# Eight of sixteen transposes moved from TensorE to 32x32 blocks on VectorE and a trip through DRAM

## The reference, cut to what matters

```python
x = x + 0.5 * ffn(layernorm(x))          # "first"
x = x + attention(layernorm(x))
x = x + 0.5 * ffn(layernorm(x))          # "second"

def ffn(x, W_fc, W_proj):
    h = square(relu(x @ W_fc.T))          # 128 -> 512
    y = h @ W_proj.T                      # 512 -> 128
    ...                                   # 5 spike steps on y, counted
    return count / 5

def attention(h, ...):                    # h has its own layer norm first
    keys, values = h @ Wk.T + bk, h @ Wv.T + bv
    w = exp((keys @ Wka.T + bka) / sqrt(128))
    w = w / cumsum(w, axis=1)
    return cumsum(w * keys, axis=1) * values
```

## Time and profile before

| what | value |
|---|---|
| median of 3 runs | 148.12 us (147.59 to 148.47) |
| the profiled execution | 147.76 us, span 146.0 us |
| TensorE | busy 140.3 us, 96% of the span |
| VectorE | busy 117.3 us, 80% |
| ScalarE | busy 113.8 us, 78% |
| GpSimd | busy 95.8 us, 66% |
| granted TensorE clock | 0.999 |

### The profile page before, as it was taken

One profiled execution on the slowest core, in us unless ns is written; L12 is line 12 of the kernel. 1 busy time (PEld: TensorE's weight loads), 2 busy tenths in 40 slices (PEclk: granted clock), 3 DMA queues, 4 the chain that ended last, 5 costly groups with the idle time before them and its releaser, 6 DMA issues.

```text
span 146.0 us, 2901 instructions
## 1 busy us (share of the span) xinstructions
PE 140.3 (96%) x945; PEld 126.1 (86%) x945; DVE 117.3 (80%) x403; ACT 113.8 (78%) x215; POOL 95.8 (66%) x141
## 2 busy tenths in 40 slices
PE   7899999999999999999999999999999999999990
PEld 7689898989989899998988989889789898979790
DVE  3894559388699989999779999999999978453674
ACT  3278877789896996959979697796796977977761
POOL 1439247929999929894998989989967952520300
PEclk9999999999999999999999999999999999999999
DMA  4975000000000000000000000020020102020222
GB/s 140 270 203 161 4 2 0 0 0 4 2 0 2 0 4 2 0 0 0 4 0 0 0 0 7 0 72 0 2 76 0 57 15 72 7 72 0 72 72 72
DMA packets 10510, 5.09 MB, mean 35 GB/s; under 512 B 1152, under 2 KB 10496, under 8 KB 10496
## 3 DMA queue, kind: packets, MB, share of 16 engines
q1 hardware_dynamic: 9808, 4.53, 10.7%
q10 hardware_dynamic: 688, 0.39, 0.9%
HBM read 2.82 MB, written 2.10 MB: 34 GB/s over the span
## 4 chain that ended last, share of the span: by engine, by line
PE 48%; DVE 25%; issue 14%; POOL 6%; DMA 3%; POOLq 1%; ACT 1%; ACTq 1%; DVEq 0%
PE work L932 19%; PE hidden L853 5%; PE hidden L857 5%; PE hidden L854 5%; POOL normed L386 4%; DMA proj_raw<-in_L_ffn_W_proj_dram 3%; DVE weight_sum L699 3%; PE work L866 2%; POOL rstd L380 2%; DVE stats L559 2%; DVE pooled L723 2%; DVE share_bank L713 2%; DVE weight_key L706 2%; DVE share_bank L718 2%; DVE stats_att L559 2%
## 5 line engine op out<-in xcount | busy, mean ns | idle before, releaser
L932 PE MATMUL work<-proj_t,square 128*128 128x128 f32 x480 | 61.2, 275 | 0.0
L932 PEld LDWEIGHTS work<-proj_t,square 128*128 128x128 f32 x480 | 58.8, 192 | 2.4 <-ACT square L460 0.4
L460 ACT ACTIVATE square<-relu 128x512 f32<-128x512 f32 x60 | 37.7, 641 | 0.7
L455 ACT ACTIVATE relu<-hidden 128x512 f32<-128x512 f32 x64 | 36.7, 606 | 0.1
L853 PE MATMUL hidden<-in_hi,fc_lo 128*128 128x512 f32 (+1 forms) x66 | 27.5, 417 | 0.1
L857 PE MATMUL hidden<-in_lo,fc_hi 128*128 128x512 f32 (+1 forms) x66 | 25.6, 387 | 0.0
L854 PE MATMUL hidden<-in_hi,fc_hi 128*128 128x512 f32 (+1 forms) x66 | 25.4, 385 | 0.0
L380 POOL TENSOR_TENSOR rstd<-var_eps,minus_half 128x4 f32<-128x4 f32 x15 | 15.2, 1012 | 14.7 <-DVE neg_mean L572 14.7
L632 DVE TENSOR_TENSOR in_lo<-work,in_hi 128x512 fp32r<-128x512 f32 x15 | 10.2, 680 | 12.3 <-ACT in_hi L451 12.3
L386 POOL TENSOR_SCALAR normed_att<-x_att,neg_mean_att,rstd_att 128x128 f32<-128x128 f32 x32 | 18.1, 578 | 0.8
L386 POOL TENSOR_SCALAR normed<-x_second,neg_mean,rstd 128x128 f32<-128x128 f32 x32 | 16.9, 540 | 0.8
(11 more groups left out here) (118 smaller groups left out, 245.8 us busy)
## 6 DMA issues: line engine op xcount, KB each, us to landing
x_first<-_attn_hidden_states_dram SPq DMA_DIRECT2D x7, 256.0 KB, 4.0
out_dram<-x_out SPq DMA_DIRECT2D x7, 256.0 KB, 2.2
out_dram<-x_out SPq DMA_DIRECT2D x4, 64.0 KB, 1.5
x_first<-_attn_hidden_states_dram ACTq DMA_DIRECT2D x1, 128.0 KB, 2.7
x_first<-_attn_hidden_states_dram SPq DMA_DIRECT2D x1, 128.0 KB, 2.4
fc_raw<-in_L_ffn_W_fc_dram SPq DMA_DIRECT2D x1, 128.0 KB, 2.8
fc_raw<-in_L_ffn_W_fc_dram ACTq DMA_DIRECT2D x1, 128.0 KB, 3.3
proj_raw<-in_L_ffn_W_proj_dram SPq DMA_DIRECT2D x1, 128.0 KB, 3.1
```

Source lines behind the costliest of these rows:

```text
L455: nc.scalar.activation(relu[j.lane][:, c, :], bank_of_hidden(j, c)[:], ACT.Relu).then_inc(relu_made[j.lane], 1)
L460: nc.scalar.activation(square[j.lane][:, c, :], relu[j.lane][:, c, :], ACT.Square).then_inc(squares_act[j.lane], 1)
L932: last = nc.tensor.matmul(work[j.lane][:, tokens], square[j.lane][:, c, tokens], proj_t[:, c, :], start=(c == 0 and t == 0), stop=(c == NC ...
```

## The change

Jobs of index 3 to 10 are no longer transposed by TensorE. When their `normed` is there, VectorE transposes its 32x32 blocks in one instruction (`ff_block_turn`) into `blocks`; SyncE stores the whole tile to DRAM (256 KB), waits until the store has landed, and issues four loads (one for each group of 32 partitions, 64 KB each, in runs of 512 bytes) which put the blocks in their places in `block_turned`. ScalarE's `in_hi` and VectorE's `in_lo` of these jobs read `block_turned` in SBUF, through a rearranged pattern, where they read `work` in PSUM. The step in which a job's layer norm is taken is now a table, `LAYER_NORM_STEP`; by it the layer norms of jobs 2 to 10 are taken one step earlier than before. Step 0 holds those of jobs 1 and 2, step 1 those of jobs 3 and 4, steps 5 and 9 hold none, and from job 11 on it is as before. GpSimd's normalisation follows the same table. The wait for the bank `work` moves from `ff_turn` to the first contraction of these jobs.

```diff
+LAYER_NORM_STEP = [-1, 0, 0, 1, 1, 2, 3, 4, 6, 7, 8, 10, 11, 12, 13, 14]
+BLOCK_TURNED = [3, 4, 5, 6, 7, 8, 9, 10]
+BLOCK_SETS = 3
+def layer_norms(i):
+    return [FeedForward(k) for k in range(len(FF_JOBS)) if LAYER_NORM_STEP[k] == i]
...
# SyncE, behind the loads of x and ahead of the stores of out
+            for k, index in enumerate(BLOCK_TURNED):
+                j = FeedForward(index)
+                sp.wait_ge(blocks_made[j.lane], blocks_before(j) + 1)
+                sp.dma_start(block_rows[k].ap(), blocks[k % BLOCK_SETS][:]).then_inc(blocks_stored[k], 16)
+                sp.wait_ge(blocks_stored[k], 16)
+                quarters = block_rows[k].ap().rearrange("(a i) (b n) -> b i a n", i=QUARTER, b=P // QUARTER)
+                if k >= BLOCK_SETS:
+                    last = FeedForward(BLOCK_TURNED[k - BLOCK_SETS])
+                    sp.wait_ge(lo_made[last.lane], last.turn + 1)
+                for q in range(P // QUARTER):
+                    part = block_turned[k % BLOCK_SETS][q * QUARTER:(q + 1) * QUARTER, :]
+                    sp.dma_start(part.rearrange("p (a n) -> p a n", n=P),
+                                 quarters[q]).then_inc(blocks_loaded[k], 16)
...
# GpSimd
-                if turn:
-                    pool.wait_ge(turned[kind], turn)
+                wait_read()
+            def wait_ff_read(j):
+                for last in feed_forward(j.index - 2):
+                    if last.by_blocks:
+                        pool.wait_ge(blocks_made[j.lane], blocks_before(j))
+                    else:
+                        pool.wait_ge(turned[j.lane], turned_before(j))
...
-                for j in feed_forward(i + 2):
+                for j in layer_norms(i + 1):
                     ff_normalise(j)
...
# ScalarE, in ff_hi
+                if j.by_blocks:
+                    k = BLOCK_TURNED.index(j.index)
+                    act.wait_ge(blocks_loaded[k], 16 * (P // QUARTER))
+                    act.wait_ge(hidden_made[j.lane], NC * j.turn)
+                    nc.scalar.activation(in_quarters(in_hi[j.lane]), by_token(block_turned[k % BLOCK_SETS]),
+                                         ACT.Copy).then_inc(hi_made[j.lane], 1)
+                    return
...
# VectorE
+            def ff_block_turn(j):
+                if j.by_blocks:
+                    dve.wait_ge(normed_made[j.lane], NT * (j.turn + 1))
+                    k = BLOCK_TURNED.index(j.index)
+                    if k >= BLOCK_SETS:
+                        dve.wait_ge(blocks_stored[k - BLOCK_SETS], 16)
+                    rows = blocks[k % BLOCK_SETS]
+                    nc.vector.transpose(rows[:].rearrange("p (b t j) -> p t b j", b=P // QUARTER, t=NT),
+                                        normed[j.lane][:].rearrange("p t (b i) -> p t b i", i=QUARTER)
+                                        ).then_inc(blocks_made[j.lane], 1)
...
+                for j in layer_norms(i):
+                    if j.index > 0:
                         ff_layer_stats(j)
-                for j in feed_forward(i + 1):
+                for j in layer_norms(i):
                     if j.index > 0:
                         ff_layer_args(j)
...
+                for j in layer_norms(i):
+                    ff_block_turn(j)
                 for b in attention(i):
                     att_sum(b)
...
# TensorE
             def ff_turn(j):
+                if j.by_blocks:
+                    return
...
+                if j.by_blocks and c == 0:
+                    pe.wait_ge(stairs_made[j.lane], STAIRS_A_JOB * j.turn)
```

More of the change, by code:

```diff
@@ L60, in __init__ @@
         self.is_last = i == len(FF_JOBS) - 1
+        self.by_blocks = i in BLOCK_TURNED
         if self.is_last:
@@ L242, in macaron_kernel @@
         normed = {k: sb(f"normed_{k}", [P, NT, P]) for k in KINDS}
+        blocks = [sb(f"blocks{k}", [P, S]) for k in range(BLOCK_SETS)]
+        block_turned = [sb(f"block_turned{k}", [P, S]) for k in range(BLOCK_SETS)]
+        block_rows = [nc.dram_tensor(f"block_rows{k}", (P, S), F32) for k in range(len(BLOCK_TURNED))]
         in_hi = [sb(f"in_hi{l}", [P, S], F32R) for l in LANES]
@@ L290, in macaron_kernel @@
         turned, hi_made, lo_made = sems("turned", KINDS), sems("hi_made", KINDS), sems("lo_made", KINDS)
+        blocks_made = sems("blocks_made", LANES)
+        blocks_stored = [sem(f"blocks_stored{k}") for k in range(len(BLOCK_TURNED))]
+        blocks_loaded = [sem(f"blocks_loaded{k}") for k in range(len(BLOCK_TURNED))]
         hidden_made, relu_made = sems("hidden_made", LANES), sems("relu_made", LANES)
@@ L313, in wait_relu, with turned_before, blocks_before, by_token @@
             engine.wait_ge(relu_made[j.lane], NC * j.turn + c + 1)
+        def turned_before(j):
+            return j.before(lambda other: not other.by_blocks)
+        def blocks_before(j):
+            return j.before(lambda other: other.by_blocks)
+        def by_token(tile):
+            return tile[:].rearrange("p (a t j) -> p t a j", a=P // QUARTER, t=NT)
+        def in_quarters(tile):
+            return tile[:].rearrange("p (t a j) -> p t a j", a=P // QUARTER, t=NT)
         def bank_of_hidden(j, c):
@@ L376, in first_inverse_deviation, with normalise @@
                                         minus_half[:, HALF_TILES:NT], ALU.pow).then_inc(rstd_made[j.lane], 1)
-            def normalise(kind, turn, source):
+            def normalise(kind, turn, source, wait_read):
                 pool.wait_ge(ln_args_made[kind], 2 * (turn + 1))
@@ L392, in ff_normalise @@
                 else:
-                    normalise(j.lane, j.turn, x_of[j.layer][j.batch])
+                    normalise(j.lane, j.turn, x_of[j.layer][j.batch], lambda: wait_ff_read(j))
             def att_normalise(b):
-                normalise("att", b, x_of["att"][b])
+                normalise("att", b, x_of["att"][b], lambda: wait_att_read(b))
             def ff_squares(j):
@@ L449, in ff_hi @@
                     return
-                act.wait_ge(turned[j.lane], j.turn + 1)
+                if j.by_blocks:
[5 more added lines that the diff above has]
+                    return
+                act.wait_ge(turned[j.lane], turned_before(j) + 1)
                 nc.scalar.activation(in_hi[j.lane][:], work[j.lane][:], ACT.Copy).then_inc(hi_made[j.lane], 1)
@@ L631, in ff_lo @@
                 dve.wait_ge(hi_made[j.lane], j.turn + 1)
+                if j.by_blocks:
+                    nc.vector.tensor_tensor(in_quarters(in_lo[j.lane]), by_token(block_turned[BLOCK_TURNED.index(j.index) % BLOCK_SETS]),
+                                            in_quarters(in_hi[j.lane]).bitcast(F32),
+                                            ALU.subtract).then_inc(lo_made[j.lane], 1)
+                    return
                 nc.vector.tensor_tensor(in_lo[j.lane][:], work[j.lane][:], in_hi[j.lane][:].bitcast(F32),
                                         ALU.subtract).then_inc(lo_made[j.lane], 1)
+            def ff_block_turn(j):
[8 more added lines that the diff above has]
+                                        ).then_inc(blocks_made[j.lane], 1)
             def att_part_lo(b):
```

5 lines of the change are left out of this document (4 added, 1 removed).

## The result

The changed kernel takes 158.17 us (median of 4 runs, 157.0 to 158.29) against 147.88 of the kernel before: a ratio of 1.067, 95% interval 1.062 to 1.073. The forecast was 152.0 with a range of 150.5 to 155.5. The direction is right, the size is not: 10.3 us were lost where 3.8 to 4 were forecast. The profiled execution took 157.0 us with a span of 155.2, 9.2 more than the span before.

A forecast was written before the change was run, and what follows sets the result against it. It took TensorE's chain to bound the kernel up to 74 us and VectorE from 75 us on, VectorE having hardly more room. Terms +2.05, +3.85, -1.3, -0.8 gave +3.8 us, forecast 152.0, range 150.5 to 155.5.

The forecast's parts named there:

- The two early losses: Steps 0 to 2: `in_lo` of job 1 late by 2.05 us, job 2's by 3.85 more through a buffer and queue loop.
- rival (c): TensorE's clock falls to its lower level after the 3.6 us early gap, costing 1.7 us: 153.7; chance 0.15.
- the clock column leaves 1.00 near 30 us: Sign of a wrong prediction: TensorE's granted clock, 1.00 in all steps before, drops after the early gap.
- `in_lo` "from SBUF instead of PSUM I take as unchanged": `in_lo` of the eight block-turned jobs on VectorE: no change in the sum, allowance 0.1 less to 0.4 more each.
- Savings of steps 3 to 9: TensorE's dropped transposes save 1.3 us in steps 3 to 5; steps 6 to 9 save 0.8 after waits.
- the shift: Lateness against the kernel before: to fall 0.44 us a step from step 3 to step 6, 4.6 at step 6's start.
- The block turn at 0.65: VectorE's block transposition: 0.65 us once in the early loop, 0.6 in a full queue.
- The lower bound: Least time of a block turn: the 361 ns cast of 384 elements scaled to 512, given as 0.43 us.
- Rival (b): VectorE is the bound and a block turn takes 1.21 us: slower still, 154.4 us; chance 0.17.
- The trip through DRAM: Store and loads of the turned blocks: about 7 us, at most 9.4, hidden behind 10.6 for job 8, cost nothing.
- The range: 150.5 to 155.5 us: low end with all eight transposes gained, upper with dear block turn and dear `in_lo`, 155.6.
- a dear `in_lo`: Upper end of the range: `in_lo` costs 0.3 us more in four jobs that meet a full VectorE queue.

The follow-up runs named there:

- Experiment 1: Changed kernel with a normed buffer of its own, one a lane, for the jobs turned by blocks: 153.13 us, ratio 1.035.
- experiment 2: Changed kernel with 14 more 128x128 matmuls into an idle bank ahead of job 2's first product: 155.97 us, ratio 1.054.
- experiment 3: Changed kernel with `in_lo` of jobs 3 to 10 reading PSUM bank `work` instead of `block_turned`, results not right: 154.68 us, ratio 1.044.
- experiment 4: Kernel before the change with `in_lo` of jobs 3 to 10 reading x in SBUF instead of `work`, results not right: 150.39 us, ratio 1.016.
- experiment 5: Changed kernel with both the own normed buffer and `in_lo` of jobs 3 to 10 from PSUM, low part wrong: 149.92 us, ratio 1.012.
- experiment 8: Kernel of experiment 1 with each block turn done twice, the first time into a spare tile: 155.0 us, ratio 1.045.
- experiment 9: Kernel of experiment 1 with job 2's layer norm moved to step 1 and job 4's to step 2: 155.29 us, ratio 1.048.

## Why the prediction was wrong

- **The two early losses (2.05 and 3.85, 5.9 together): right in mechanism.** Measured 1.4 at the third product of job 1 and 5.4 at that of job 2, so 1.4 and 4.0. The first is smaller because GpSimd finished job 2 at 15.94, not 16.5. `in_lo` of job 1 started at 16.11 (16.8 forecast), that of job 2 at 27.59 (28.1), and the idle time ended by GpSimd's `normed` before the second block turn is there, 4.75 us. Experiment 1 shows the loop by undoing it.
- **TensorE's clock, rival (c): it happened, and the sum had nothing for it.** The price was 1.7; it is 1.7 in the trace, 1.6 by experiment 2 counted from the start of the table and 2.2 by its median. The gap of 3.6 us was forecast and measured at 3.76, so what was mis-sized is the chance of 0.15. The prediction had named this as a sign of being wrong: the clock column leaves 1.00 near 30 us. A gap as long had no row in the kernel before to be read against. The Trainium skill (TensorE: Matmul & The Clock Gate, Part 1) says that an idle array falls back to the lower clock, and the trace agrees: 0.51 behind the gap, 1.00 where work fills it.
- **`in_lo` "from SBUF instead of PSUM I take as unchanged": the step that failed.** The sum had nothing for it, and 3.0 to 3.5 us hang on its place (experiment 3; 2.7 in the other direction, experiment 4). The pass grew from 0.69 to 1.09 in the mean. That is the 0.4 which the prediction allowed as its worst, but it allowed it for about four jobs, 1.6 us, and 1.2 in the upper bound; six jobs grew, by up to 0.8. It was priced by VectorE's own row alone; the other party, GpSimd's two-operand passes, 1.27 us each and right beside `in_lo` in six of the eight steps, was left out.
- **Savings of steps 3 to 9, 2.1: too large.** With both big losses out, experiment 5 shows 0.7 to 0.8, nearly all of it from the transposes of jobs 3 and 4. From step 3 to step 6 the shift was to fall by 0.44 a step; it rose. That the block turns use up the rest in VectorE's full queue is argued from experiment 8, not shown.
- **The block turn at 0.65: right** (0.71, with the next instruction 0.63 later). The lower bound was misreckoned: 361 ns for 384 elements scale to 0.48 us for 512, not 0.43; nothing hangs on it. Rival (b) in its form (an expensive block turn) is out; VectorE is the bound all the same, through `in_lo`.
- **The trip through DRAM, nothing: right.** About 6 us against 7 forecast, and nothing waits for it.
- **The range.** It added the dear block turn and a dear `in_lo`, but not the clock, which came on top. Counted from the start of the table the start lost 5.7, the clock 1.6 and `in_lo` 3.0, and 0.7 were saved: 9.6 against 9.5 measured. The median is at 10.3; the executions that make it have the mean clock of 0.978 and a span 1.0 to 1.3 longer than the profiled one. No trace of one of them was kept, so where exactly that time goes is open.

## What to carry to other kernels

When an operand moves from PSUM to SBUF, ask what GpSimd does in the same microseconds: a two-operand pass that had one operand in PSUM ran undisturbed, and with both in SBUF it and GpSimd's two-operand passes held each other up, the one that began second waiting for the other. When work is pulled ahead by a step, follow its buffer through every queue, and look for a loop in which an engine can only leave one step after another engine has entered the next. A gap on TensorE that is forecast should be priced twice, for the idle time and for the slow matmuls behind it. And before two executions are compared to half a microsecond, line them up behind the first loads.

## What the runs showed that I had not expected

- Fourteen matmuls into an idle bank, placed in a gap, made the kernel 2.2 us faster without moving the operand that TensorE waited for.
- VectorE's 32x32 transposition of 128x512 float32 takes 0.69 to 0.71 us, as long as any plain pass, with patterns in runs of 32.
- A load of 64 KB in runs of 512 bytes lands in 1.8 us at best and 2.0 in the median, the median of a 256 KB store.
- The contention goes either way: beside `in_lo`, `guess_share` took 1.28 us where it had begun first and 1.75 where it began second.
- TensorE's clock fell behind one gap of 3.76 us and also behind two short waits with little work between them (experiment 9), but not behind a gap of 1.08 us (experiment 1).
